# The last batch's eight returned-row loads: one behind a mask in place of two behind each of the first four masks

## The reference

```python
xn = _layernorm(x, axis=-1)
q, k = _l2norm(q), _l2norm(k)                      # 16 heads of 8
attn = softmax(where(causal, -max, einsum('bhid,bhjd->bhij', q, k) * 8.0))
attn_out = einsum('bhij,bhjd->bhid', attn, v) @ Wo
for e in range(8):                                 # top 2 experts of each token
    h = gelu(xn @ W1[e].T + b1[e]); y = h @ W2[e].T + b2[e]
    ffn_out += y * w_e[..., None]
out = x + attn_out + ffn_out
```

## Time and profile before

| what | value |
|---|---|
| median of 3 runs | 680.59 us (680.46 to 680.67) |
| profiled execution, its own time | 680.41 us |
| its span in the trace | 678.7 us |
| PE busy | 615.8 us (91%) |
| DVE busy | 465.7 us (69%) |
| ACT busy | 449.9 us (66%) |
| POOL busy | 418.0 us (62%) |

### The profile page before, as it was taken

The page is one execution under the profiler, slowest core; times in us unless marked ns, Lnnn a source line. Parts: engine busy times, 40 slices in busy tenths (PEclk is TensorE's granted clock), DMA queues, the critical chain, the costliest instruction groups (busy, mean ns, idle before and its releaser), DMA issues. The chain is left out here.

```text
span 678.7 us, 21454 instructions
## 1 busy us (share of the span) xinstructions
PE 615.8 (91%) x7417; PEld 411.7 (61%) x7417; DVE 465.7 (69%) x1312; ACT 449.9 (66%) x689; POOL 418.0 (62%) x584
## 2 busy tenths in 40 slices
PE   2877558999999999999999999999999999999965
PEld 2755323444444438999999999999984444444423
DVE  7799986766676776445545446777566687878826
ACT  3999546888888884444444444444449888888854
POOL 6355627778777787775600027677737777677771
PEclk9899968999999999999999999999999999999989
DMA  5997685655445578855432335444536375556621
GB/s 160 297 288 228 185 248 111 109 108 104 115 115 118 125 126 199 206 143 143 108 88 71 73 88 120 112 115 118 120 78 104 84 137 116 121 124 139 122 68 32
DMA packets 186592, 89.36 MB, mean 132 GB/s; under 512 B 115456, under 2 KB 176032, under 8 KB 186400
## 3 DMA queue, kind: packets, MB, share of 16 engines
q1 hardware_dynamic: 178192, 70.70, 44.7%
q0 software_dynamic: 8336, 17.84, 9.8%
HBM read 30.17 MB, written 32.24 MB: 92 GB/s over the span
## 5 line engine op out<-in xcount | busy, mean ns | idle before, releaser
L812 ACT ACTIVATE prob<-psum 128x1536 f32<-128x1536 f32 x192 | 267.2, 1453 | 64.0 <-PE psum L922 62.2
L822 ACT ACTIVATE prob<-psum,prob 128x256 f32<-128x256 f32 x284 | 117.5, 471 | 132.2 <-PE psum L1062 129.3
L648 POOL DMA_INDIRECT rows<-slot_y,idx x128 | 130.4, 1019 | 46.1 <-issue 27.2
L650 POOL DMA_INDIRECT slot_x<-rows,slots x128 | 128.2, 1001 | 36.1 <-issue 30.4
L954 PE MATMUL psum<-prob,v 128*18 128x448 f32 (+3 forms) x2048 | 137.9, 388 | 8.6 <-POOL prob L664 8.6
L664 POOL TENSOR_SCALAR_AFFINE_SELECT prob<-prob 128x384 f32<-128x384 f32 (+2 forms) x224 | 104.8, 477 | 62.6 <-ACT prob L812 60.5
L1074 PEld LDWEIGHTS psum<-prob 128*128 128x128 f32 x1136 | 137.8, 192 | 3.6
L1074 PE MATMUL psum<-prob 128*128 128x128 f32 x1136 | 138.1, 275 | 0.0
L1062 PE MATMUL psum<-xs,prob 128*128 128x256 f32 x568 | 134.8, 380 | 0.6 <-DVE xs L1468 0.4
L1062 PEld LDWEIGHTS psum<-xs,prob 128*128 128x128 f32 x568 | 102.5, 190 | 12.4 <-DVE xs L1468 0.6
L954 PEld LDWEIGHTS psum<-prob,v 128*18 128x18 f32 x2048 | 48.8, 98 | 97.0 <-issue 75.9
(11 more groups left out here) (159 smaller groups left out, 661.3 us busy)
## 6 DMA issues: line engine op xcount, KB each, us to landing
slot_y<-xs SPq DMA_DIRECT2D x71, 128.0 KB
xs<-in_L_attn_x SPq DMA_DIRECT2D x16, 256.0 KB, 4.1
prob<-in_L_ffn_W SPq DMA_DIRECT2D x16, 256.0 KB, 3.6
xn_rows<-prob SPq DMA_DIRECT2D x16, 256.0 KB, 2.7
xn_cols<-xts SPq DMA_DIRECT2D x16, 256.0 KB, 3.0
xt<-xn_cols SPq DMA_DIRECT2D x16, 256.0 KB
rows<-xn_rows SPq DMA_DIRECT2D x16, 256.0 KB, 3.5
out<-acc SPq DMA_DIRECT2D x15, 256.0 KB
```

What stands on the lines that cost most here:

```text
L648: pool.indirect_dma_start(rows[:, j, c, t, :], None, done, where).then_inc(moved[j], 16)
L650: pool.indirect_dma_start(slot_x, where, halves_of_rows[:, j, 0, t, :], None).then_inc(moved[j], 16)
L812: act.activation(prob[:, KEPT[k], :], score[k % 2], ACT.Exp, scale=SCALE / UP ** 2)\
L822: act.activation(hs[:, s, c, :], psum[:, 2 * s + c // 2, (c % 2) * FT:(c % 2 + 1) * FT], ACT.Gelu, bias=ws[:, s, B1C + c:B1C + c + 1]).the ...
```

## The change

The last batch loses its own order. It then takes the order of batches 9 to 14: one load behind each of the masks 0, 1, 3, 4, 6, 7, 9 and 10. The loads themselves, the masks, and the waits of every other engine stay as they are.

```diff
                     order = [[BACKS.index(u)] if u in BACKS else [] for u in range(UN)]
                     if known(b, 0):
                         order = [[], [], [], [], [], [0], [1, 2], [3], [4, 5], [6], [7], []]
-                    if last:
-                        order = [[0, 1], [2, 3], [4, 5], [6, 7]] + [[]] * (UN - 4)
                     for o in order[k]:
                         move(b, par, o, second)
```

## The result

The changed kernel takes 675.57 us (median of 4, 674.97 to 676.25), the kernel before 680.53 us on the same occasion: a ratio of 0.9921, 95% interval 0.9909 to 0.9933, 5.0 us faster. The profiled execution took 674.97 us with a span of 673.2 us. 675.0 was forecast.

The account below looks back on a forecast made before the run. In the last batch, PE waits 5.12 us for POOL's mask 3, delayed by loads. Winning 4.92 there plus 1.22 to chunk 8, minus 0.53 for the landing, gives 5.60 us: median 675.0, range 674.2 to 677.3.

Parts of the forecast that it names:

- The wait before chunk 1: Last batch: PE's idle time before chunk 1 falls from 5.12 to 0.2 us, winning 4.92 us there.
- The way to mask 9: Last batch, chunk 1 to mask 9 at full clock: PE waits 0.8 us before chunk 3; mask 9 starts at 659.42.
- The batch before the last, shifted by one offset: POOL's times in the last batch, read from the previous batch's same order, 19.32 us later: mask 3 ends at 651.60.
- The landing: End of the last batch: DVE's combines must now wait until load 7 has landed, costing 0.53 us of the gain.
- The term taken from a scatter: Load 7's landing: 1.34 us past its issue's end, taken from the last send of stage three.
- Who releases `finish`: End of the last batch: DVE's six combines release `finish` at 666.24; PE would be done at 665.71.
- that rival: Last batch: the clock falls anyway after PE's idle times; gain only 3.3 us, 677.3 us; chance 0.15.
- the signs that I had named for being wrong: Changed profile: clock near 0.5 after 654, DVE's wait for loads beyond 2.5 us, or `finish` still waiting for PE.
- The sum: Start of `finish`: 666.24 instead of 671.84, 5.60 us earlier, from 4.92 plus 1.22 minus 0.53; median 675.0 us.
- The slower rival: Load 7's landing: from 6.9 us past the issue's end the change loses, at 10.3 giving 683.9 us; chance 0.04.

Follow-up runs that it names:

- e11_early_again: Second run of the changed kernel with each load of the last batch one or two masks earlier, load 0 ahead of mask 0: 673.91 us, ratio 0.9911.
- e1_again: The changed kernel run again without any edit, for its time and a second profile: 674.34 us, ratio 0.9917.
- e9_third: The changed kernel run a third time without any edit: 674.83 us, ratio 0.9927.
- e2_fill_end: The changed kernel with five extra matmuls, result overwritten, between chunks 7 and 8 of the last batch: 675.48 us, ratio 0.9927.
- e5_last_late: The changed kernel with load 7 of the last batch behind mask 11 in place of mask 10: 676.17 us, ratio 0.9947.
- e4: The changed kernel with the last batch's eight loads one behind each of masks 0 to 7: 675.84 us, ratio 0.9935.
- e6: The changed kernel with each last-batch load one or two masks earlier, load 0 ahead of mask 0, none behind masks 10 and 11: 673.80 us, ratio 0.9898.
- e10: Second run of the changed kernel with the last batch's loads one behind each of masks 0 to 7: 676.27 us (one run).
- e7_no_loads: The changed kernel without the last batch's eight loads, its combines reading batch 13's rows, so the output is incomplete: 673.51 us, ratio 0.9905.

## Why the prediction was right

- **The wait before chunk 1.** Forecast 0.2 us in place of 5.12; it was 0.39 to 0.40. Masks 2 and 3 took 1.23 us together instead of the 1.05 read from the earlier trace rows. Chunk 1 started 6.48 us after the first exponential, 6.28 were forecast.
- **The way to mask 9.** Forecast was one more wait, 0.8 us before chunk 3: it was 0.63 to 0.64. Mask 9 started 14.17 us after the first exponential, against 14.05 forecast, and mask 11 was done after 18.38, against 18.30. The batch before the last, shifted by one offset, was a good template for POOL only up to mask 5 (0.2 us). At mask 9 that offset would have been 1.2 us late; the forecast took mask 9 from chunk 4 and the exponentials instead, and that held.
- **The landing.** The term taken from a scatter, 1.34 us past the issue's end, was 0.3 to 0.4 too small: 1.61, 1.64, 1.64, 1.69 and 1.74 us were measured where DVE waited the whole of it, and 1.76 in e11_early_again, where it waited the last 0.18 us. The store of batch 14's output isn't the reason: in e11 it is issued at 662.84, after the load's bytes had moved (661.8 to 662.4). By the Trainium skill's figure ("DMA: Bandwidth & Descriptors", section "Anatomy of one DMA — SWDGE (gpsimd) path") it would have been 2.15, an estimate that is 0.4 to 0.5 too large if it counts from the issue's end, as the forecast had it, and 0.4 to 0.65 too small if it counts from the issue's start (2.58 to 2.80 us were measured from there). With 1.7 in the sum `finish` comes after 21.2, where e1_again and e9_third have 21.12 and 21.07. That closeness holds two more differences of opposite sign: the issue of load 7 ended 0.15 us later than forecast (17.80 against 17.65 us after the first exponential), and the six combines took 1.58 us to `finish` instead of 1.88.
- **Who releases `finish`.** DVE, as forecast, in e1_again, e9_third, e2_fill_end and e5_last_late. In the first profile of the changed kernel it was PE, because the clock had fallen. I had that rival, but placed it in the middle of the batch behind the waits on masks 3 and 5; it struck before chunk 8, in one execution of three, and cost 22.06 - 21.1 = 0.96 us, not 2.3, since 0.7 us of the slow chunks lay beside the combines. So two of the signs that I had named for being wrong stood in the first profile, a clock near 0.5 and `finish` waiting for PE. The second was to say that the landing is shorter than 0.8 us, and it was 1.61: a slow chunk 8 gives the same sign.
- **The sum.** 5.60 us were forecast to be won between the first exponential and `finish`; 5.35 and 5.40 were measured at full clock, 4.41 with the low one. The medians give 5.0, 5.75 and 5.3 us. That the profiled span came out at 673.2 beside a forecast 673.1 is two differences that cancel: the batch began 1.11 us early, and `finish` came 1.19 us late within it. From `finish` to the end of the span it was 6.86 us as forecast, within 0.13 (6.88, 6.99 and 6.95 in the three profiles).
- **The slower rival**, a landing of more than 6.9 us, had no part in it: none took more than 1.76.

## What to carry to other kernels

An engine that issues indirect DMAs between short steps on which others wait should spread them, and e4, e5 and e6 show how finely it matters: count the issues ahead of each step that someone waits for, and leave the last ones early enough for their landing. Look for the idle time that the issuing engine already has, here ahead of the batch's first mask; with one load moved there and the others a mask or two earlier all eight were free. And a profile of one execution should be taken twice before a term is blamed on it: the same program had its last chunks at 3.55 and at 1.92 us.

## What the runs showed of the hardware

- The granted clock after a short idle time varies from execution to execution of one program. Behind 1.85 us of idle time on PE, before chunk 8, it was 0.54 once and 1.00 twice; behind 1.38 us, before chunk 1, 0.52 once and 1.00 once. It stayed at 1.00 behind 2.47 us in e10, so the length of the one idle time doesn't decide. In one profile each, it averaged 0.53 behind the 5.12 us of the stall, and 1.00 with 3.84 us of matmuls put into that stall and 1.59 us idle remaining. What makes the difference between equal executions is open.
- The last projections, behind `finish`, kept PE busy for 1.39 us at 1.00 in the kernel before, and for 2.41 us at 0.50 in e9_third, there after 2.41 us of idle time.
- A mask on POOL beside DVE's combines took 0.65 us in one execution and 1.78 in another of the same program.
- The distance between the first exponentials of two successive batches varies for one and the same batch, with the same instructions. For batch 13 it was 19.00 us in the first profile of the changed kernel (606.11 to 625.11) and in e9_third, 19.78 in the kernel before (606.26 to 626.04), 19.81 in e1_again and 20.17 in e7_no_loads. That accounts for 0.78 of the 1.11 us by which the last batch began earlier. Its cause wasn't looked for, and whether it also makes the spread of the medians isn't shown.
